# Layer norm inside two attention layers: averaging products, logarithm and exponential against turned tokens, per-partition moments and a power on 128x4

## What is computed

```python
x = x + attn0(layernorm(x))              # L0 attention, diagonal of a column softmax
x = x + ffn0(layernorm(x))               # two layers, below
x = x + attn1(layernorm(x))              # 16 heads, causal
x = x + moe(layernorm(x))                # 8 experts, top 2, and a shared one

def _layer(x, wqkv, qs, ksc, wo, lg, lb, w1, b1, w2, b2):   # twice inside ffn0
    ...                                  # shift_token, local attention, windows of 64
    x = x + o @ wo
    h = shift_token(x)
    mu = h.mean(-1, keepdims=True)
    var = h.var(-1, keepdims=True)
    h = (h - mu) / jnp.sqrt(var + 1e-05) * lg + lb
    a, g = jnp.split(h @ w1 + b1, 2, axis=-1)
    x = x + (a * gelu(g)) @ w2 + b2
```

## Time and profile before

| | |
|---|---|
| median of 3 runs | 2063.85 us (2063.61 to 2066.46) |
| the profiled execution's own time | 2061.38 us |
| its span, first to last instruction | 2059.3 us |
| mean granted clock of TensorE | 0.91 of full |
| busy: PE, PEld | 1616.5, 941.5 us |
| busy: DVE, ACT, POOL | 1121.5, 1015.8, 605.5 us |
| DMA | 80.7 MB, mean 39 GB/s |

### The profile page before, as it was taken

How to read it: one execution, slowest core, us unless ns; L and a number is a source line. 1 busy time by engine, 2 the same in 40 slices (tenths; PEclk the granted TensorE clock), 3 DMA queues, 4 the chain that set the end, 5 groups by cost and what they waited for, 6 DMA issues and landing times.

```text
span 2059.3 us, 32978 instructions
## 1 busy us (share of the span) xinstructions
PE 1616.5 (78%) x11554; PEld 941.5 (46%) x11632; DVE 1121.5 (54%) x2562; ACT 1015.8 (49%) x2297; POOL 605.5 (29%) x400
## 2 busy tenths in 40 slices
PE   1666688986889768895889868897699957898579
PEld 1334244553546435562445535463355625455235
DVE  3443492746646474644927466464837449274514
ACT  1435246653657327472466536573374724665041
POOL 5624060513315051420605033150515106051000
PEclk9787789997999889997999979999899979999689
DMA  4010200112002120113101120021201130011301
GB/s 127 19 23 1 59 23 2 50 51 62 21 1 65 50 47 21 28 46 77 31 2 49 51 62 21 1 65 51 47 21 34 49 79 20 2 49 44 62 2 51
DMA packets 37330, 80.69 MB, mean 39 GB/s; under 512 B 6766, under 2 KB 22638, under 8 KB 33760
## 3 DMA queue, kind: packets, MB, share of 16 engines
q1 hardware_dynamic: 37136, 78.22, 14.8%
HBM read 54.74 MB, written 8.78 MB: 31 GB/s over the span
## 4 chain that ended last, share of the span: by engine, by line
PE 43%; DVE 17%; ACT 14%; issue 13%; POOL 10%; DMA 1%; SPq 1%; DVEq 0%; POOLq 0%; ACTq 0%
PE ps L324 37%; PE ps L329 6%; ACT work L718 4%; DVE cmax L1032 4%; POOL work L1178 4%; ACT big L785 4%; POOL small L1155 3%; DVE small L934 2%; POOL work L1189 2%; DVE work L903 2%; ACT L807 1%; ACT L718 1%; ACT big L807 1%; DVE work L902 1%; DVE small L910 1%
## 5 line engine op out<-in xcount | busy, mean ns | idle before, releaser
L324 PE MATMUL ps<-bxt,mw 128*128 128x512 f32 x576 | 276.6, 604 | 3.7 <-ACT big L807 3.7
L324 PE MATMUL ps<-maskb,identb 128*128 128x128 bf16 (+1 forms) x1106 | 228.7, 239 | 27.9 <-ACT work L718 16.4
L718 ACT ACTIVATE work<-ps,pbias,small 128x128 f32<-128x128 f32 x512 | 226.1, 473 | 48.0 <-DVE pbias L938 47.5
L1155 POOL TENSOR_TENSOR brs<-bmv,consts 128x4 f32<-128x4 f32 x16 | 3.2, 202 | 754.3 <-DVE bmv L843 754.3
L324 PE MATMUL ps<-wqkv,h 128*128 128x512 f32 x384 | 199.4, 651 | 30.9 <-ACT v L680 11.0
L1032 DVE TENSOR_REDUCE cmax<-ps 128x1 f32<-128x384 f32 (+3 forms) x352 | 204.3, 630 | 29.7 <-PE ps L324 29.6
L1178 POOL TENSOR_TENSOR work<-work 128x1024 f32<-128x1024 f32 x64 | 150.7, 2354 | 232.2 <-DVE work L903 231.6
L1155 POOL TENSOR_TENSOR small<-small,consts 128x8 f32<-128x8 f32 x128 | 208.2, 1640 | 2.6 <-DVE small L912 2.6
L324 PE MATMUL ps<-pk,pq 96*128 96x512 bf16 (+3 forms) x512 | 139.6, 329 | 79.6 <-DVE cmax L1032 54.7
L329 PE MATMUL ps<-ident,work 128*128 128x128 f32 x1056 | 169.4, 307 | 40.0 <-DVE work L979 12.9
L785 ACT ACTIVATE big<-ps 128x512 f32<-128x512 f32 x320 | 163.9, 634 | 57.0 <-PE ps L324 56.9
(11 more groups left out here) (162 smaller groups left out, 2611.0 us busy)
## 6 DMA issues: line engine op xcount, KB each, us to landing
mw<-in_experts SPq DMA_DIRECT2D x72, 384.0 KB, 3.0
pk<-scr_parts SPq DMA_DIRECT2D x48, 192.0 KB
pq<-scr_parts SPq DMA_DIRECT2D x144, 64.0 KB
v<-v SPq DMA_DIRECT2D x16, 512.0 KB, 4.5
v<-v SPq DMA_DIRECT2D x16, 384.0 KB, 5.8
scr_parts<-big SPq DMA_DIRECT2D x8, 768.0 KB, 3.9
xin<-in_x SPq DMA_DIRECT2D x8, 256.0 KB, 4.4
out<-x SPq DMA_DIRECT2D x8, 256.0 KB, 3.1
```

The costliest lines, as they stand in the source:

```text
L324: return nc.tensor.matmul(o, a, b, start=start, stop=stop, skip_group_check=True)
L718: i = nc.scalar.activation(pr[:, m, a, p, :], fb[2 * (m % 2) + a][:, p * P:(p + 1) * P], ACT.Exp, bias=pbias[:, m, k:k + 1], scale=rn[:, m ...
L1155: return nc.gpsimd.tensor_tensor(out, x, consts[:, k:k + 1].broadcast_to([x.shape[0], x.shape[1]]), op)
```

## The change

Both norms of the local layers take the other form. The residual `hs` is turned (four transposes, part `lt.l`) into PSUM bank 1 with tokens on the partitions; VectorE takes statistics of it there; GpSimd adds eps and takes the power on 128x4 (part `lr.l`, behind `pt1.l`); VectorE normalises from PSUM into `fxn`; TensorE turns it back (part `lx.l`, bank 2); ScalarE applies gain and bias from PSUM. The mean and variance products, the square, Ln, Exp, two VectorE passes, the matrix `mean_w` and the three buffers `dc`, `dsq`, `drs` go.

```diff
@@ tensor
-                    yield f"mean.{l}"
+                    yield f"lt.{l}"
                     pe.wait_ge(l_h1.sem, l_h1.at(s, l + 1))
-                    mm(fb[1], mean_w[:, :], hs).then_inc(l_mean.sem, 1)
-                    yield f"var.{l}"
-                    pe.wait_ge(l_dsq.sem, l_dsq.at(s, l + 1))
-                    mm(fb[2], mean_w[:, :], dsq).then_inc(l_var.sem, 1)
+                    turn_tiles(fb[1], lambda tt: hs[:, tt * P:(tt + 1) * P]).then_inc(l_ht.sem, 1)
+                    yield f"lx.{l}"
+                    pe.wait_ge(l_xn.sem, l_xn.at(s, l + 1))
+                    turn_tiles(fb[2], lambda tt: fxn[:, tt, :]).then_inc(l_xt.sem, 1)
@@ scalar
-                    yield f"mean.{l}"
-                    act.wait_ge(l_dc.sem, l_dc.at(s, l + 1))
-                    nc.scalar.activation(dsq, dc, ACT.Square).then_inc(l_dsq.sem, 1)
-                    yield f"var.{l}"
-                    act.wait_ge(l_var.sem, l_var.at(s, l + 1))
-                    nc.scalar.activation(drs, fb[2][:, :], ACT.Ln, bias=consts[:, 0:1]).then_inc(l_ve.sem, 1)
-                    act.wait_ge(l_ve.sem, l_ve.at(s, l + 1))
-                    nc.scalar.activation(drs, drs, ACT.Exp, scale=-0.5).then_inc(l_drs.sem, 1)
                     yield f"hn.{l}"
-                    act.wait_ge(l_dn.sem, l_dn.at(s, l + 1))
-                    nc.scalar.activation(hn, dc, ACT.Identity, bias=lnb[:, l:l + 1], scale=lng[:, l:l + 1]).then_inc(l_hn.sem, 1)
+                    act.wait_ge(l_xt.sem, l_xt.at(s, l + 1))
+                    nc.scalar.activation(hn, fb[2][:, :], ACT.Identity, bias=lnb[:, l:l + 1], scale=lng[:, l:l + 1]).then_inc(l_hn.sem, 1)
@@ vector
-                    yield f"mean.{l}"
-                    dve.wait_ge(l_mean.sem, l_mean.at(s, l + 1))
-                    dve.wait_ge(l_h1.sem, l_h1.at(s, l + 1))
-                    tt_(dc, hs, fb[1][:, :], ALU.subtract).then_inc(l_dc.sem, 1)
-                    yield f"var.{l}"
-                    dve.wait_ge(l_drs.sem, l_drs.at(s, l + 1))
-                    tt_(dc, dc, drs, ALU.mult).then_inc(l_dn.sem, 1)
+                    turned = fb[1].rearrange("p (a b) -> p a b", a=NT)
+                    yield f"lt.{l}"
+                    dve.wait_ge(l_ht.sem, l_ht.at(s, l + 1))
+                    spread(s, turned, fst, fv)
+                    moments(s, l + 1, fst, fmv, l_mv, fv)
+                    yield f"lx.{l}"
+                    normalise(s, l + 1, turned, fxn, fmv, frs, l_lr, l_xn)
@@ gpsimd
-            nc.gpsimd.memset(mean_w[:, :], 1.0 / P)
...
                     yield f"pt1.{l}"
                     normalise_probs(3)
+                    yield f"lr.{l}"
+                    rstd(s, l + 1, l_mv, fmv, frs, fp, l_lr)
```

More of the change, by code:

```diff
@@ L49 @@
 ORDER = {
[L50 to L58, removed]
+    "tensor": "BBFFFFFFFFFBBFBFBBFFBBBBFFFBFFBBBBBBFBBFBBBFFBFBFBBBBBFBBBFBBBBBBBBFBBBFFFBBFBFBBBBBBFFBBBFBBFBBBBBB"
+        "BBBBFBBBBBBBBBBBBBBBBBBFBBBBFFFFFFBBBFBBBBBBBFBBBBFBBBBFBBFFBBBFBBBBBBBBBFBBBBFFBBBBBFBFFFFFBBBBBFBB"
+        "BFBBBFBBBFBBBFFFFFFFBFFBFBBBBBFBFFFFFFFF",
+    "scalar": "BBFFFFFFFFFFFFFFFFFFFFFFFFFFFFFFFFFFFFBBFBBBFFBBBBBBBBBBBBBBBBBBBBBBBBBBBFBFFFBBBBBBBBBBFFBFFFBFFFBB"
+        "BFBBBFFBFBBBFFBFFBFFBBFFFBBFFFFFBFFFFFFBBBFFFF",
+    "vector": "BBFFBBBBFFFFFBFFFFFFBBBFFBFBFFFFBFFFFBBBBFBBBBBBBBBFBBFFBBFBBBFBFBBBFBBFBBFBBBBBFFFBBBFBBBFBFFFFFFFF"
+        "FFBBBBFFBBBFBBBBBBBFBFFFBBBFBBFFBFFBFFBBBFFBBBFBFFBBFBFFFFFFBBFBBFBBBFFFFF",
+    "gpsimd": "BFFFFFFFFFFFFFFFFFFFFFFFBFFFFFFFFFFFFFFF",
+    "sync": "FBFBBBBBBBFBBBB",
 }
@@ L166, in program @@
         identb = sb("identb", [P, P], BF16)
-        mean_w = sb("mean_w", [P, P])
         maskb = sb("maskb", [P, 2 * T + 2 * P], BF16)
@@ L214, in program @@
         gel = [work1[0:HT, HC * T + i * T:HC * T + (i + 1) * T] for i in range(2)]
-        dc, dsq, drs = (work1[:, (5 + i) * T:(6 + i) * T] for i in range(3))
         cs_in = work1[:, 0:2 * NT * 2 * DH].rearrange("p (z a j d) -> p z a j d", z=2, a=NT, j=2)
@@ L280, in program @@
         l_wo, l_h1 = sig("l_wo", LAYERS), sig("l_h1", LAYERS)
-        l_mean, l_dc, l_dsq, l_var = sig("l_mean", LAYERS), sig("l_centred", LAYERS), sig("l_centred_sq", LAYERS), sig("l_var", LAYERS)
-        l_ve = sig("l_var_log", LAYERS)
-        l_drs, l_dn, l_hn = sig("l_rstd", LAYERS), sig("l_dn", LAYERS), sig("l_hn", LAYERS)
+        l_ht, l_mv, l_lr = sig("l_h_turned", LAYERS), sig("l_moments", LAYERS), sig("l_rstd", LAYERS)
+        l_xn, l_xt, l_hn = sig("l_xn", LAYERS), sig("l_xn_turned", LAYERS), sig("l_hn", LAYERS)
         l_g, l_a, l_gelu, l_hg = sig("l_g", LAYERS * 3), sig("l_a", LAYERS * 3), sig("l_gelu", LAYERS * 3), sig("l_hg", LAYERS * 3)
@@ L286, in program @@
         f_ft, f_x2 = sig("f_out_turned", 1), sig("f_x2", 1)
-        fv, fp = chain("front_vector", 6 + 4 * LAYERS), chain("front_gpsimd", 2)
+        fv, fp = chain("front_vector", 6 + 5 * LAYERS), chain("front_gpsimd", 2 + LAYERS)
         b_stats, b_rstd, b_xn, b_tp, b_xt = (sig(n, 2) for n in ("b_stats", "b_rstd", "b_xn", "b_turned", "b_xt"))
```

## The result

The changed kernel takes 2077.35 us (median of four runs, 2075.69 to 2077.99); the kernel before, measured beside it, 2064.95 (2063.61 to 2066.46). The ratio is 1.0059, interval 1.0041 to 1.0076: it is slower by 12 us. Forecast were 2034 us, a range that ends at 2058, and 0.84 for faster. Both size and sign are wrong.

What follows compares the result with a forecast made beforehand. From about 545 us in an iteration, TensorE's work plus stalls was the limit. 3.3 + 1.3 less 0.6 gives 4.0 us; 7 x 4.0 + 2.2 = 30 off 2061.4, plus 2.5 for the median: 2034 us, range 2016 to 2058.

Steps and rivals of the forecast that it cites:

- 4.79 - 2.4 + 0.86 = 3.3 us: Layer 0's norm, per iteration: four TensorE stalls of 4.79 us become 2.4, and 0.86 us of work is saved.
- The remaining waits of 2.4 us: TensorE's later waits per iteration: exponential 0.4, copy of v 0.4, back half's norm 0.65, its copy then router 0.9 us.
- the back half's norm, behind the rotary sum: TensorE's wait for the back half's second norm, its power queued behind GpSimd's rotary sums: 0.65 us.
- ScalarE's 4.51 us per norm: ScalarE loses two table loads (2.57 us) and three passes (1.95 us) per norm, 16 times.
- the loads from 17 to 11: ScalarE's table loads per iteration: four fewer by the norm, two fewer by regrouping (2.6 us).
- the front alone: Sequence 0's front half running alone: layer 1's norm takes 7.0 us for 8.1; with layer 0, 2.2 us saved.
- 0.86 us per norm: TensorE's work: 1.71 us of products removed, 0.86 of transposes added, so 0.86 less per norm.
- bound of 0.5 us per norm for a PSUM operand: VectorE's high-end extra for reading PSUM, 0.06 us on each of eight passes; the forecast took 0.
- The tail: Layer 1's norm among the last two expert products: TensorE saves 0.86 of work and some 0.4 of waiting, 1.3 us.
- C: Rival: back half's second norm and router become the path once waits pass 6.5 us; slower, 2078 us; chance 0.09.
- D: Rival: transposes let TensorE's clock fall to 1.2 GHz before the feed forward, 7.7 us per iteration, 2088 us; chance 0.02.
- marks of a wrong forecast: Iteration at 238 or more, back power wait above 2 us, TensorE idle before first down product, clock below 1.00 after 555.

Runs made afterwards that it cites:

- the old head and the new tail: New norm; order of before up to layer 0's second value product, order of the change from there: 2055.33 us, 0.9954 of the kernel before.
- four fillers: New norm in the old order plus four unused constant products ahead of each of two long TensorE waits at an iteration's start: 2023.97 us, 0.9809 of the kernel before.
- the two edits between the waits: Changed kernel with two added constant products (2052.73 us), or with layer 1's second q/k product moved ahead of the turn of the normalised tokens (2054.22 us).
- eight fillers: New norm in the old order plus eight unused constant products at each of two waits at an iteration's start: 2043.71 us, 0.991 of the kernel before.
- the new order with fillers: Changed kernel with layer 1's second q/k product moved ahead, four constant products at each of two start waits, one before the router: 2046.54 us, 0.9927.
- the root ahead of the sum: Changed kernel with the power of the back half's second norm ahead of layer 1's second rotary sum on GpSimd: 2078.8 us, 1.0076 of the kernel before.
- the new head with the old tail: New norm; order of the change up to layer 0's second value product, order of before from there: 2040.72 us, 0.9889 of the kernel before.

## Why the prediction was wrong, point by point

**The step that failed** is the iteration's "4.79 - 2.4 + 0.86 = 3.3 us". It was laid out with durations at full clock and it priced a wait by its own length. Three terms in it failed:

- *The remaining waits of 2.4 us.* Those between 600 and 610 were put at about 1.95 (0.4, 0.65, 0.9, the last including the router's copy) and measure 3.50. The largest miss is "the back half's norm, behind the rotary sum": 0.65 forecast, 1.48 measured, as the normalising took 1.83 us for 1.11. The two exponential tails before the value products of layer 0, forecast as one wait of 0.4, are 1.04 and 0.60:

```profile
568.09 2.36 PE L321 MATMUL ps<-big,va 128*32 128x512 f32 x32 [1.04 <-ACT big L774]
...
576.14 2.36 PE L321 MATMUL ps<-big,va 128*32 128x512 f32 x32 [0.60 <-ACT big L774]
```

- *The clock,* not in the sum at all: 6.8 us at half clock, about 3.4 us per iteration, as much as the whole forecast of 3.3.
- *The head of the order,* costed at nothing: 8.5 us by its own run, whose iterations take 237.1 us in place of 235.5.

In the sum of waits from layer 0's value products to the iteration's end the change saves nothing: 10.1 us before, 10.6 after, 9.6 with the new norm in the old order, 11.2 with the old head and the new tail. (The first and the last trace show 11.06 and 11.90. There 0.94 and 0.70 us lie where a weight load stands without its product, a record that is missing and not a wait.) The order that was to hide the stalls brings in more than it removes.

**The norm's own terms hold where they can be read.** In the old order the norm gives 2032.17 and 235.5 us per iteration. That this is nearly what was forecast for the whole change (2034, 236) is luck: the forecast had the stalls going by the new order. ScalarE's 4.51 us per norm is right: that kernel has 944.9 us, 1016 less 72, without the regrouping. So are the loads from 17 to 11, the front alone (6.9 for 7.0, though its terms, 5.0, 1.1 and 0.69 to 0.81, add up to 6.8 to 6.9), and leaving out the drain of 1380 ns that the Trainium skill (ScalarE: Activation LUTs, "What ACT_TABLE_LOAD costs") gives; the trace shows nothing between load and pass.

**TensorE's busy time** tells nothing of its term: 0.86 us per norm was to take 14 us off, and with the new norm in the old order it is 1617.0 against an incomplete 1616.5, so this term stays unchecked by itself.

**VectorE** came to +27 us for +17. Its bound of 0.5 us per norm for a PSUM operand would give 8 more and was the right one to take for the normalising passes (1.36 for 1.11, 16 times: 4 us). Another 5 us is the stretching beside GpSimd: the back half's 64 normalising passes sum to 22.8 us, and to 17.8 in the old order.

```profile
L838 DVE TENSOR_SCALAR bxn<-x,bmv,brs 128x128 f32<-128x128 f32 x64 | 22.8, 418 | 25.2 <-POOL brs L1143 25.2
L838 DVE TENSOR_SCALAR fxn<-ps,fmv,frs 128x128 f32<-128x128 f32 x64 | 21.8, 403 | 12.6 <-POOL frs L1143 12.6
```

**The tail** was to give 1.3 us, 0.4 of it in waits. The wait of 1.22 us for the expert sum, forecast to stay, is 0.78, but the waits behind 620 us sum to 4.9 us before and 5.0 after, so the 0.4 isn't there.

**The rivals.** C named the right place (VectorE between the second rotary product and the first gated pass) and asked for 6.5 us of waiting there before the kernel would be slower. TensorE's waits there are 2.15 (1.48 and 0.67), 3.50 with the two ahead of them. They were enough together with the clock behind them and the head, since C priced waits by length too. D had the clock and gave it 0.02, for a wrong cause: transposes. They are all in the kernel with the old order, whose clock stays at 1.00 in that part. What spoke for D was the rule of the Trainium skill (TensorE: Matmul & The Clock Gate, "Part 4: PE-mode transpose") that transposes don't count as activity in the same way; that part of this kernel doesn't bear it out. What TensorE did before the clock fell, in the iteration shown, was to wait four times in 10 us. Of the things named as marks of a wrong forecast, two came up: an iteration above 238, and a clock below 1.00 after 555 us.

**What stays open.** Why the clock falls in the changed kernel and not with the old head, where the four waits are equal to 0.01 us, isn't settled. Of the new tail's 3.2 us per iteration (238.7 for 235.5) the waits explain 1.6; the rest isn't itemised.

The lengths of the iterations bear on both. From the second iteration to the sixth, ten of the twelve kernels here keep within 0.5 us of one length: 235.5 us (the new norm in the old order, without and with four fillers), 239.0 (the old head with the new tail, the two edits between the waits, eight fillers, the new order with fillers), 242.4 (the changed kernel, the root ahead of the sum) or 256.0 (the old norm in the new order). The kernel before has 239.1 and once 241.8; only the new head with the old tail wanders, from 235.8 to 238.5. Five unlike edits share 239.0, and the first three lengths lie 3.4 to 3.5 us apart. So an iteration's time doesn't follow the waits tenth by tenth, and a sum of small terms, as in the prediction, can't be confirmed term by term from it. No run shows what makes the steps.

The back alone moves between 156.8 and 162.1 us over these kernels though its instructions don't change but for the fillers; its mean clock over that stretch is 0.86 and 0.82 at these two ends, and 2.7 of the 12 us lost stand there.

## What to carry to other kernels

When a change brings a new operation and a new order made for it, time the operation in the old order first: here the two together lose 12 us and the operation alone gains 32. Price a cluster of short waits on TensorE also by the clock behind it, and try an independent product in the wait, but no longer than the wait: two products between the waits gained 24.6 us here, and eight in place of four at the iteration's start lost 20. Before reading a sum of waits from a trace, compare the products with the weight loads, since a missing record looks like a wait.

## What the runs showed of the hardware that was not expected

- A stretch at 1.2 GHz can follow waits of no more than 0.67 to 1.48 us, 3.5 us together; it lasted 6.8 us, with TensorE busy throughout. Two products of 128x512 in those waits kept the clock at 1.00.
- VectorE's normalising from SBUF slows down while GpSimd runs a tensor pass: four passes of 128x128 take 1.11 us alone, 1.83 beside a GpSimd pass of 1.04 us, and 3.87 beside one of 2.34 followed by one of 1.04. The excess (0.72 and 2.76) is most of the time that the two run side by side (0.98 and 3.27). Moving GpSimd's work ahead for VectorE's sake can make VectorE later.
- Statistics over 128x128 cost nearly the same from PSUM as from SBUF (0.89 and 0.87 us for four).
